# Eight dense experts per token replaced by expert lists in DRAM, blocks of 500 gathered rows and indirect adds

## The reference

```python
x = x + relu(adj @ (item @ W_item.T + b_item) + (layernorm(x) @ W_user.T + b_user))
xf = layernorm(x)
probs = softmax(xf @ gate_w + gate_b)                # 10000 x 8
cw = probs where the expert is among the token's top 2, else 0
x = x + sum over e of cw[:, e] * (gelu(xf @ W1[e] + b1[e]) @ W2[e] + b2[e])
```

## Time and profile before

| what | value |
|---|---|
| median of 3 runs (lowest, highest) | 1702.58 us (1701.86, 1703.87) |
| profiled execution, its own time | 1701.72 us |
| its span, first to last instruction | 1699.9 us |
| mean granted TensorE clock | 0.999 of 2.4 GHz |

### The profile page before, as it was taken

How to read it: one execution, slowest core, us unless ns; L and a number is a source line. 1 busy time by engine, 2 the same in 40 slices (tenths; PEclk the granted TensorE clock), 3 DMA queues, 4 the chain that set the end, 5 groups by cost and what they waited for, 6 DMA issues and landing times.

```text
span 1699.9 us, 26881 instructions
## 1 busy us (share of the span) xinstructions
PE 1669.3 (98%) x7485; PEld 1352.6 (80%) x7485; DVE 1465.4 (86%) x2285; ACT 1231.9 (72%) x1596; POOL 69.6 (4%) x63
## 2 busy tenths in 40 slices
PE   6999999999999999999999999999999999999997
PEld 5877888888888888888878787878888888888864
DVE  5988989898988888888888898989898989898874
ACT  4777777777777777777777777767777777777764
POOL 1000000000000000000000000000000000000000
PEclk9999999999999999999999999999999999999999
DMA  9998777777778787777777787878787787787810
GB/s 330 344 313 274 259 256 248 262 251 258 253 250 263 248 265 246 261 238 257 252 257 252 251 258 253 254 251 262 255 254 260 246 262 250 256 259 247 265 38 13
DMA packets 124638, 423.73 MB, mean 249 GB/s; under 512 B 14261, under 2 KB 19894, under 8 KB 124618
## 3 DMA queue, kind: packets, MB, share of 16 engines
q1 hardware_dynamic: 120456, 415.41, 75.2%
q10 hardware_dynamic: 3314, 5.71, 0.9%
q0 software_dynamic: 848, 2.36, 0.4%
HBM read 418.31 MB, written 5.12 MB: 249 GB/s over the span
## 4 chain that ended last, share of the span: by engine, by line
PE 93%; DVE 2%; DMA 2%; ACT 2%; issue 0%; ACTq 0%; SPq 0%; DVEq 0%
PE acc L758 20%; PE acc L760 20%; PE acc L759 20%; PE ps_z L831 4%; PE ps_z L832 4%; PE ps_y L790 4%; PE ps_z L833 4%; PE ps_y L784 3%; PE ps_y L786 3%; PE ps_y L785 3%; PE ps_w L841 2%; DMA raw<-in_adj_main 2%; PE acc L776 1%; PE ps_x L766 1%; DVE a_lo L541 1%; PE ps_g L808 1%
## 5 line engine op out<-in xcount | busy, mean ns | idle before, releaser
L541 DVE TENSOR_TENSOR a_lo<-raw,a_hi 128x1000 fp32r<-128x1000 f32 (+1 forms) x800 | 930.8, 1183 | 135.0 <-ACT a_hi L389 130.1
L389 ACT ACTIVATE a_hi<-raw 128x1000 fp32r<-128x1000 f32 (+1 forms) x800 | 801.3, 1026 | 226.0 <-PE acc L760 194.1
L758 PE MATMUL acc<-a_hi,h_hi 128*128 128x500 f32 x1580 | 644.8, 408 | 8.0 <-DVE a_lo L541 6.9
L760 PE MATMUL acc<-a_hi,h_lo 128*128 128x500 f32 x1580 | 615.5, 390 | 0.0
L759 PE MATMUL acc<-a_lo,h_hi 128*128 128x500 f32 x1580 | 613.1, 388 | 0.0
L758 PEld LDWEIGHTS acc<-a_hi,h_hi 128*128 128x128 f32 x1580 | 297.6, 188 | 79.5 <-issue 20.8
L759 PEld LDWEIGHTS acc<-a_lo,h_hi 128*128 128x128 f32 x1580 | 297.4, 188 | 66.2 <-issue 12.9
L760 PEld LDWEIGHTS acc<-a_hi,h_lo 128*128 128x128 f32 x1580 | 296.5, 188 | 60.8
L454 ACT ACTIVATE g_sb<-ps_z,b_sb 128x500 f32<-128x500 f32 x320 | 198.5, 672 | 88.8 <-DVE gs_lo L678 83.4
L678 DVE TENSOR_TENSOR gs_lo<-g_sb,gs_hi 128x500 fp32r<-128x500 f32 x240 | 151.8, 674 | 38.9 <-PE ps_y L786 37.6
L669 DVE TENSOR_TENSOR g_sb<-ps_w,g_sb 128x500 f32<-128x500 f32 x240 | 151.2, 672 | 7.8 <-ACT g_sb L454 7.8
(11 more groups left out here) (121 smaller groups left out, 1059.6 us busy)
## 6 DMA issues: line engine op xcount, KB each, us to landing
raw<-in_adj_main SPq DMA_DIRECT2D x780, 500.0 KB, 4.4
xr_sb<-in_xR SPq DMA_DIRECT2D x20, 250.0 KB
x_sb<-in_xT SPq DMA_DIRECT2D x20, 250.0 KB, 2.7
out<-r_sb ACTq DMA_DIRECT2D x20, 250.0 KB, 3.8
items<-in_itemT SPq DMA_DIRECT2D x13, 384.0 KB, 6.3
g_sb<-in_w POOLq DMA_DIRECT2D x4, 250.0 KB, 7.4
raw<-in_adj_rem SPq DMA_DIRECT2D x20, 31.2 KB, 2.7
r_sb<-in_w POOLq DMA_DIRECT2D x2, 250.0 KB, 7.8
```

What stands on the lines that cost most here:

```text
L389: nc.scalar.activation(a_hi[q][0:rows, 0:cols], raw[s][0:rows, 0:cols], ACT.Copy).then_inc(hi_ready, 1)
L541: nc.vector.tensor_tensor(a_lo[q][0:rows, 0:cols], raw[s][0:rows, 0:cols], val(a_hi[q][0:rows, 0:cols]), ALU.subtract).then_inc(lo_ready, 1)
L758: nc.tensor.matmul(acc[:, 0:T], w_hi, m_hi, start=(k == 0), stop=False)
L760: last = nc.tensor.matmul(acc[:, 0:T], w_lo, m_hi, start=False, stop=(k == KT))
```

## The change

The gate still runs for every tile in the pass after it. What it gives is now a place for each token in the lists of its two experts:

- `rows_sb` holds, for each of 125 x 4 tokens, a row of RW = 140 words: the 128 normalised numbers, the 8 weights, the token's number. Five small products with a triangle of ones (`T_PREFIX`) count how many tokens ahead go to the same expert; VectorE makes from it the row numbers `dest_at`. GpSimd then writes each token's row (560 bytes) twice into the DRAM tensor `lists`, by 8 indirect transfers of 125 rows (`dispatch`).
- x1 is now made in token rows, and is stored to the output at once (position `A_STORE`), by ScalarE's queue.
- A block is 500 rows of one expert's list. Which one is next is chosen on VectorE (`pick_block`) from the fill of the lists; SyncE reads the choice into a register and loads the 500 rows; GpSimd copies that expert's weights (both parts, 128 x 1024 numbers) and biases out of a table. TensorE turns the rows (4 transposes), 6 products up, 6 down, 4 transposes back to token rows; ScalarE and VectorE do Gelu and splits as before; VectorE scales by the weight of each token; GpSimd adds the rows to the output by 4 indirect transfers with an add (512 bytes a row).
- Passes 1 to 5 carry no blocks. Passes 6 to 19 carry two blocks each (28), the walk over the positions after the last pass carries two more, and LATE = 17 blocks come after all lists are complete: 47 blocks in all, in place of 160 expert tiles. The late blocks alternate between two sets of buffers, `weights(n + 2)` stands ahead of `add(n)` on GpSimd's queue, and each `add` waits until all earlier adds have landed.
- All experts use the split weights (`w_table`), and the plain fp32 products, the spreading product and the bias products are gone.

The core of the diff (its constants, the new queue work, and the order of the late blocks):

```diff
+CAP = N + T
+PER = 2
+FIRST = 6
+LOOPED = PER * (NB - FIRST)
+WAITING = 2 * N - T * (LOOPED + PER)
+LATE = E + (WAITING - E) // T
+NLATE = LOOPED + PER
-STARTS = (27, 31, 35, 39, 44, 49, 54, 59)
+T_TURN, T_BACK, T_GATE, T_PREFIX = 2, 8, 12, 23
+A_RELU, A_STORE, A_NORM, A_EXP, A_USER = 2, 9, 11, 16, 38
+V_X1, V_NORM, V_LOGITS, V_PROB, V_COMPARE, V_RANK, V_MASK, V_DEST = 5, 8, 15, 17, 18, 20, 21, 26
+S_ROWS = 11
+S_LOAD = (8, 19)
+B_TURN, B_UP, B_DOWN, B_ROWS = (8, 20), (13, 25), (19, 31), (24, 36)
+B_HI, B_GELU, B_GHI, B_KEEP = (11, 23), (16, 28), (17, 29), (22, 34)
+B_PICK, B_LO, B_META, B_GLO, B_SCALE = (0, 12), (11, 23), (12, 24), (17, 29), (27, 39)
...
 # SyncE
+            def load_block(count, s, rows, back, tiles):
+                sp.wait_ge(picked_ready, count(1, -1))
+                at = sp.value_load(picked[s][0:1, 0:1], min_val=0, max_val=SPARE)
+                sp.wait_ge(scattered, tiles)
+                since(sp, x_turned, count(1, back - 1))
+                since(sp, meta_ready, count(2, back - 1))
+                sp.dma_start(rows[0:TQ, 0:Q * RW], list_blocks[at]).then_inc(rows_landed[s], 16)
...
 # GpSimd
+            def dispatch(i):
+                pool.wait_ge(t_normed, i)
+                pool.wait_ge(row_ready, 2 * i)
+                pool.wait_ge(dest_ready, i)
+                for k in range(2):
+                    for q in range(Q):
+                        j = k * Q + q
+                        pool.indirect_dma_start(
+                            lists, bass.IndirectOffsetOnAxis(dest_at[:, j:j + 1], 0),
+                            rows_sb[0:TQ, q * RW:(q + 1) * RW], None).then_inc(scattered, 16)
+            def weights(n):
+                s = n % 2
+                pool.wait_ge(picked_ready, n + 1)
+                at = pool.value_load(picked[s][0:1, 1:2], min_val=0, max_val=E - 1)
+                since(pool, down_done, n - 1)
+                since(pool, y_kept, n - 1)
+                nc.gpsimd.tensor_copy(w_block[s][:, :, :], w_table[:, :, bass.ds(at * WW, WW)]).then_inc(w_copied, 1)
+                nc.gpsimd.tensor_copy(b_block[s][:, :], bias_sb[:, bass.ds(at * NBIAS, NBIAS)]).then_inc(w_copied, 1)
+            def add(n, tiles):
+                pool.wait_ge(y_ready, n + 1)
+                since(pool, added, 16 * Q * n)
+                pool.wait_ge(x1_stored, 16 * tiles)
+                yr = work(n)["yr"]
+                for q in range(Q):
+                    pool.indirect_dma_start(
+                        out, bass.IndirectOffsetOnAxis(tok_at[meta_slot(n)][:, q:q + 1], 0),
+                        yr[0:TQ, q * D:(q + 1) * D], None, compute_op=ALU.add).then_inc(added, 16)
...
+            for i in range(FIRST, NB + 1):
+                n = PER * (i - FIRST)
+                weights(n)
+                if n:
+                    add(n - 1, i - 2)
+                tail(i)
+                if i < NB:
+                    user(i)
+                weights(n + 1)
+                add(n, i - 1)
+                dispatch(i)
+            weights(NLATE)
+            add(NLATE - 1, NB - 1)
+            weights(NLATE + 1)
+            for n in range(NLATE, BLOCKS):
+                if n + 2 < BLOCKS:
+                    weights(n + 2)
+                add(n, NB)
...
 # ScalarE, late blocks
+                n = NLATE + t
+                if 0 <= t < LATE:
+                    gelu(numbered(n), work(n), reuse(n), n % 2)
+                if 0 <= t + 1 < LATE:
+                    split_rows(numbered(n + 1), work(n + 1), reuse(n + 1))
+                if 0 <= t < LATE:
+                    split_g(numbered(n), work(n), reuse(n))
+                if 0 <= t - 1 < LATE:
+                    keep(numbered(n - 1), work(n - 1), reuse(n - 1), (n - 1) % 2)
...
 # VectorE, late blocks
+                if 0 <= t + 1 < LATE:
+                    read_meta(numbered(n + 1), work(n + 1), (n + 1) % 2, meta_slot(n + 1), 4)
+                    split_rows(numbered(n + 1), work(n + 1))
+                if 0 <= t < LATE:
+                    split_g(numbered(n), work(n))
+                if 0 <= t - 2 < LATE:
+                    scale(numbered(n - 2), work(n - 2), reuse(n - 2), meta_slot(n - 2))
+                if 2 <= t + 3 < LATE:
+                    pick_block(numbered(n + 3), (n + 3) % 2, NB)
...
 # TensorE, late blocks
+                if 0 <= t < LATE:
+                    up(numbered(n), work(n), n % 2)
+                if 0 <= t + 1 < LATE:
+                    turn_rows(numbered(n + 1), work(n + 1), (n + 1) % 2)
+                if 0 <= t - 1 < LATE:
+                    down(numbered(n - 1), work(n - 1), (n - 1) % 2)
+                if 0 <= t - 2 < LATE:
+                    to_rows(numbered(n - 2), work(n - 2))
```

738 lines of the change are left out of this document (414 added, 324 removed).

## The result

The changed kernel takes 1901.13 us (median of 4 runs, 1895.82 to 1904.85), the kernel before 1702.22 us beside it (4 runs, 1700.36 to 1703.87). The ratio is 1.1167, 95% interval 1.1136 to 1.1197: slower by 11.7%. The forecast of 1659 us had the wrong sign, and its range (1590 to 1785 us) did not hold the time. The profiled execution spans 1900.5 us, 244.5 more than the 1656 of the prediction's sum.

What follows compares the result with a forecast made beforehand. It took TensorE's products to bound the kernel before the change, 81.2 us of a pass's 81.69. First pass 94 + 5 x 61 + 14 x 71 + 263 behind the loop = 1656 us of span, forecast 1659, range 1590 to 1785 us.

Steps and rivals of the forecast that it cites:

- The price of an indirect transfer: GpSimd's time for each indirect transfer, taken as 1.1 us, between 0.536 us (plain transfer) and 1.917 us (slowest instruction).
- Rival 2: Behind the loop, GpSimd's queue of four serial adds per late block sets the time; a loss from 1.65 us each; chance 0.24.
- The gate's chain: Behind the last pass: the last tile's gate, from relu to row numbers, with nothing to hide it, some 27 us.
- The rate of the loads: In the loop: 21.0 MB a pass without blocks, 22.6 with, at 359 or 304 GB/s: 58.5 to 69 and 63 to 74 us.
- I take 61 for passes 1 to 5: Each pass without blocks takes 61 us, between 58.5 and 66.
- rival 3: In the loop, 125-row transfers use only 5 of 16 engines: 6.5 us a pass more, a 77 us pass, 1743 us; chance 0.18.
- They cannot all be full at once: Passes with blocks: TensorE 65, VectorE 63, loads 63 to 74 us stand close, so 71 us, between 65.5 and 77.
- The power behind weights and adds: Behind the last pass, the last gate's power stands behind `weights` and `add` on GpSimd's queue, within the chain's 27 us.
- Up to 2 us each this stays hidden: Within a pass, adds and dispatch land before SyncE asks for them, if an indirect transfer takes up to 2 us.
- The clock: In late blocks TensorE's products start at 1.2 GHz after idling; half an up costs 0.55 us more, cycle 13.0 us.
- The shared port: VectorE and GpSimd lock each other out; two weight copies a pass cost VectorE up to 3 us, 66 in place of 63.
- rival 1: Everything at its low price: TensorE-bound passes of 66 us, indirect transfers of 0.54 us, 1544 us with both; chance 0.18.

Runs made afterwards that it cites:

- e1: The changed kernel with its transfers of 125 rows (x rows, list loads, x1 store) split into 112 and 13 rows: 1837.67 us.
- e12: e1 with four matrix buffers in place of five: 1981.38 us; a pass without blocks took 76.3 us, against 64.8 in e1.
- e8: e1 with one product in place of three in the experts, up and down: 1817.81 us; a pass with blocks 75.7 us, against 75.1 in e1.
- e7: e1 with adds that carry 16 of 128 columns (64 bytes a row): 1829.31 us; a pass with blocks 75.2 us, against 75.1 in e1.
- e16: e15 with the adds cut to 64 bytes a row: 1743.18 us; a pass with blocks 72.1 us, against 71.9 in e15.
- e14: e8 with six VectorE operations a pass, the low-part differences, cut from 500 columns to one: 1785.57 us; a pass with blocks 74.2 us.
- e15: e14 with relu for gelu on ScalarE, written straight into the high part, whose copy is cut to one column: 1747.65 us.
- e2: The changed kernel with the tail's power ahead of weights and add on GpSimd's queue: 1870.64 us.
- e10: Against a kernel joining e1, e2, e5 and an earlier last dispatch (1764.95 us): blocks' last steps two positions later, second scaling unmoved; 1821.13 us.
- e6: The changed kernel with 40 products that nothing reads issued on TensorE with each late block: 1895.67 us.
- e13: Against a kernel joining e1, e2, e5 and an earlier last dispatch: list loads on GpSimd's queue, a pass's first ahead of its first power; 1758.03 us.
- e3: The changed kernel with add's indirect transfers writing their rows instead of adding them: 1820.96 us.
- e5: The changed kernel with four weight buffers for late blocks, weights(n + 3) ahead of add(n), and six slots for token numbers: 1831.61 us.

## Why the prediction was wrong

The sum had three groups of terms, and each was too small; the excess behind the loop alone (1659 + 100 = 1759 us) or that of the passes alone (1659 + 144 = 1803 us) would have made the change a loss.

- **The price of an indirect transfer** was one number, 1.1 us. For the scatter in the tail it was nearly right: 1.18, and 1.49 from start to start. For the add it was 2.31. The step that failed is the bound from above: 1.65 us was named as the point of loss, and then one value was taken for two forms. Rival 2 had the place, the mechanism and the sign. Fifteen cycles (adds from 1617.38 to 1873.68 us) took 256 us in place of 195. That is 61 of the tail's 100 us; the last in-loop add with the dispatch took 21 us in place of 13 (8 more), the way from there to the first late add 30 in place of 16 (14 more, a further group of adds among it), and the last two blocks with their landing 27 in place of 12 (15 more). The gate's chain, 30 us against 27, was nearly right.
- **The rate of the loads.** The step "I take 61 for passes 1 to 5" came from the 359 GB/s of the kernel before's first 45 us. After the change passes 1 to 5 ran at 308 GB/s. e1 explains 3.5 us of the 7.3: 125 rows on 5 engines, which is rival 3's mechanism at half its price; why half, no run shows. The remaining 3.8 us I put down to the five buffers' round trip: e12 shows that the passes go by it, not that it is all of the 3.8. The prediction priced bytes by a rate and never asked how long a buffer is away; before, TensorE's 81.7 us hid a trip of 8 us (10.2 us were there for it).
- **"They cannot all be full at once".** The prediction added 10 us to a pass for the blocks (71 against 61), and the runs show 10.4. So the difference was right, but by another mechanism than the one named: not TensorE (e8), whose 65 us were its lower end, and not the adds' bytes (e7, e16; those of the scatter and the list loads were in every run), but in part operations of ScalarE and VectorE that stand in order between the splits which empty the buffers (e14, e15). When a pass lives on a round trip, an operation on the trip costs time even on an engine that is busy for 79% (DVE 869.89 of 1101 us).
- **The power behind weights and adds** was listed for the tail, where it costs once; in the loop it cost 0.9 to 1.7 us a pass (e2) as long as the uneven loads were there too.
- **Hidden from SyncE.** "Up to 2 us each this stays hidden" held barely: the wait for the scatter was 16.9 us in 10 of the 14 passes. e10 shows the price when it is not hidden.
- **The clock.** Half an up at 1.2 GHz was to cost 0.55 us a cycle. The term stood in the right place and was too small: the three cycles of e6 whose products up ran at 2.4 GHz were 0.65 us and, with the products down at it too, 1.3 to 1.5 us shorter.
- **The shared port.** With shapes apart the split L676 took 1209 ns from 500 to 1400 us, and L541 1197 in the same stretch before: 12 ns, 0.5 us a pass. The four normalisations of the x rows (L704) took 507 ns each, and 343 before (L575): 0.7 us more. Up to 3 us had stood in the prediction. The Trainium skill (SBUF — State Buffer, Who interferes with whom) has the two engines lock each other out; on VectorE's side no more than this shows here. GpSimd's side, which the prediction did not price, pays more. Its indirect transfers from 436 to 1537 us; between the bars stand busy us and mean ns:

```profile
L473 POOL DMA_INDIRECT out<-yr_sb,tok_at x108 | 260.1, 2409 | 334.1 <-DVE yr_sb L846 307.0 <-issue 27.1
L453 POOL DMA_INDIRECT lists<-rows_sb,dest_at x112 | 167.9, 1499 | 37.1 <-issue 33.8 <-DVE picked L815 3.4
```

So in the loop an add takes 2.41 us and a scatter 1.50, against 2.00 and 1.18 in the tail. Whether VectorE's operations are what holds them up stays open: no run takes those away.

- **Slips that moved nothing.** The "20 multiplications and rests" of VectorE are 28 by the earlier trace rows (60 + 60 + 20 in five passes); their 17.7 us are right. The "1.06 MB" of rival 3 are 1.08 by the terms of its own sum of the loads. "About 1590 with the one or the other" in rival 1 is 1589 with the short passes and 1614 with the cheap transfers.

What is right is the division of work: TensorE's busy time fell by 180 us, the loop is 96.5 us shorter (relu to relu 1442.6 against 1539.1 us), and the tail gives it back three times over, 297 us more than the 66 of before.

What stays open: some 6 us of a pass with blocks are left in e15 over one without (71.9 against 65.9). They are not the adds' bytes; leaving out products (e8) or taking the list loads out of SyncE's queue (e13) did not shorten a pass by more than 0.4 us. That two or three causes share them (the other operations of the blocks, the list loads ahead of matrix loads in one queue, SyncE's wait of 34.6 us between 500 and 1400 us in e15) was not tried in one run.

## What to carry to other kernels

A gather and scatter that saves matrix products has two prices that the busy shares do not show: a chain of late work whose cycle is set by a serial queue of small transfers, and each form of transfer in it has to be priced by itself. When the busiest engine is relieved, ask first how long one buffer's round trip is (issue, landing, each engine that reads it), and divide it by the number of buffers for the time of one position; here that was the next bound, and operations put between the readers added about half their own length. A transfer whose row count divides badly over 16 engines cost 3.5 us a pass once the loads had no slack. And a mean clock over a stretch does not tell at which clock the products that others wait for ran: look at their own rows.

## What the hardware did that was not expected

- In the tail an indirect transfer of 125 rows that adds keeps GpSimd for 2.00 us, one that writes for 1.18 us, and 0.30 us lie before the next; 64 bytes a row cost the adding form as much of GpSimd as 512 (e3, e7). In the loop they take 2.41 and 1.50 us.
- From the start of a group's last add until the next group may start, having landed, are 5.6 us (e5): longer than the store of 250 KB took before (3.8 us).
- 40 idle products per late block raise the mean granted clock from 0.68 to 0.91, yet in eleven of fourteen late cycles the products up still run at 0.50 of 2.4 GHz; the three cycles in which they run faster are 0.65, 0.65 and 1.5 us shorter (e6).
